# Turning the qkv weight on TensorE instead of on VectorE, in the first attention of a fused block

## The reference, cut to what matters

```python
# _L0_cond_ref: a low-rank adapter per batch entry
Bx  = jnp.einsum('bni,bri->bnr', x, B[adapter_ids])
out = jnp.einsum('bnr,bor->bno', Bx, A[adapter_ids])
# _L0_attn_ref: 32 query heads in 8 groups, each with its key and value head
qkv  = jnp.einsum('sbh,ph->sbp', tokens, weight_qkv)      # p = 8 groups * (4 + 2) heads * 128
scores = jnp.einsum('bhsd,bhtd->bhst', q, k) * scale      # causal, s and t run over 8
attn = jax.nn.softmax(scores, axis=-1)
out  = jnp.einsum('bhst,bhtd->bhsd', attn, v)
out  = jnp.einsum('sbe,he->sbh', out, weight_proj)
x = x + out
```

## Time and profile before

| | |
|---|---|
| median of 3 runs | 1549.35 us (1543.15 to 1550.29) |
| the profiled execution's own time | 1550.29 us |
| its span, first to last instruction | 1548.6 us |
| busy: PE | 1485.0 us, 96% |
| busy: DVE / ACT / POOL | 78% / 56% / 57% |
| mean granted TensorE clock | 0.989 of full speed |
| DMA | 133.37 MB, 169701 packets, of which 119187 under 512 B |
| first stage | from the start to about 290 us |

### The profile page before, as it was taken

The page is one execution under the profiler, slowest core; times in us unless marked ns, Lnnn a source line. Parts: engine busy times, 40 slices in busy tenths (PEclk is TensorE's granted clock), DMA queues, the critical chain, the costliest instruction groups (busy, mean ns, idle before and its releaser), DMA issues.

```text
span 1548.6 us, 26991 instructions
## 1 busy us (share of the span) xinstructions
PE 1485.0 (96%) x8792; PEld 1269.1 (82%) x8792; DVE 1208.1 (78%) x2700; ACT 866.8 (56%) x2260; POOL 878.9 (57%) x1231
## 2 busy tenths in 40 slices
PE   6699999989999999999999999999999999999997
PEld 4588888778888888888888888888888888888885
DVE  5688887778778887788788888878788888777865
ACT  2322232356666666666666666666666666666641
POOL 1111343256666666766676676667666766676521
PEclk9899999999999999999999999999999999999999
DMA  8988765222212221222122222212221222211102
GB/s 184 230 169 173 171 137 148 80 83 72 79 55 71 69 77 57 72 68 71 57 81 71 69 68 75 71 55 73 80 69 57 74 74 59 88 57 50 41 27 82
DMA packets 169701, 133.37 MB, mean 86 GB/s; under 512 B 119187, under 2 KB 128787, under 8 KB 169563
## 3 DMA queue, kind: packets, MB, share of 16 engines
q1 hardware_dynamic: 152098, 97.56, 23.9%
q0 software_dynamic: 16464, 33.85, 7.4%
q10 hardware_dynamic: 1000, 0.23, 0.1%
HBM read 107.47 MB, written 7.34 MB: 74 GB/s over the span
## 4 chain that ended last, share of the span: by engine, by line
PE 86%; SPq 5%; ACT 2%; issue 2%; DVE 2%; POOL 1%; DMA 1%; POOLq 0%; DVEq 0%
PE ps_t L932 14%; PE ps_o L746 11%; PE ps_o L748 11%; PE ps_o L747 10%; PE ps_b L746 5%; PE ps_b L748 5%; PE ps_b L747 5%; PE ps_q L748 4%; PE ps_q L747 4%; PE ps_q L746 4%; PE ps_a L746 3%; PE ps_a L747 3%; PE ps_a L748 3%; SPq L454 2%; PE ps_a L795 2%
## 5 line engine op out<-in xcount | busy, mean ns | idle before, releaser
L1418 ACT ACTIVATE sm<-sm,mn 128x640 f32<-128x640 f32 x256 | 211.4, 826 | 233.6 <-DVE mn L1908 227.1
L1784 DVE TENSOR_TENSOR pT_lo<-ps_t,pT_hi 128x512 fp32r<-128x512 f32 x320 | 220.2, 688 | 114.5 <-ACT pT_hi L1341 101.5
L629 POOL DMA_INDIRECT kraw<-in_L_cond_k_cache_dram,idx_a x200 | 197.4, 987 | 89.2 <-issue 75.7
L1341 ACT ACTIVATE pT_hi<-ps_t 128x512 fp32r<-128x512 f32 x320 | 188.5, 589 | 85.1 <-PE ps_t L932 82.2
L629 POOL DMA_INDIRECT vraw<-in_L_cond_v_cache_dram,idx_a x200 | 198.6, 993 | 59.6 <-issue 59.3
L932 PE MATMUL ps_t<-ident,sm 128*128 128x128 f32 x1280 | 196.4, 276 | 3.5 <-DVE sm L1920 1.5
L932 PEld LDWEIGHTS ps_t<-ident,sm 128*128 128x128 f32 x1280 | 148.7, 141 | 51.6 <-DVE qT_lo L1784 17.5
L646 POOL TENSOR_TENSOR z<-pairs_p,zl 128x128 f32<-128x128 f32 x160 | 57.9, 402 | 193.6 <-DVE pairs_p L1637 193.6
L746 PE MATMUL ps_o<-wo_lo,oT_hi 128*128 128x512 f32 x256 | 118.0, 461 | 12.4 <-ACT kvown L1345 10.8
L746 PE MATMUL ps_o<-pT_lo,v_hi 128*128 128x512 f32 x320 | 129.8, 405 | 0.0
L748 PE MATMUL ps_o<-pT_hi,v_hi 128*128 128x512 f32 x320 | 125.5, 392 | 0.0
(11 more groups left out here) (257 smaller groups left out, 4305.6 us busy)
## 6 DMA issues: line engine op xcount, KB each, us to landing
fv<-st SPq DMA_DIRECT2D x128, 128.0 KB, 2.4
tab<-tab_scratch SPq DMA_DIRECT2D x64, 256.0 KB
wblk<-n_L_attn_weight_qkv_dram SPq DMA_DIRECT2D x32, 384.0 KB
wpraw<-_L_attn_weight_proj_dram SPq DMA_DIRECT2D x8, 1024.0 KB, 5.6
mask<-mask_scratch SPq DMA_DIRECT2D x64, 128.0 KB
wtile<-in_L_cond_Wq_dram SPq DMA_DIRECT2D x28, 256.0 KB
wtile<-in_L_cond_Wo_dram SPq DMA_DIRECT2D x28, 256.0 KB
kraw<-in_L_cond_k_cache_dram,idx_a POOLq DMA_INDIRECT x200
```

The lines of the kernel that those rows point to most:

```text
L629: pool.indirect_dma_start(raw[:, par, c, :], None, rows_d, bass.IndirectOffsetOnAxis(idx[:, k:k + 1].bitcast(U32), 0)).then_inc(arrived[pa ...
L1341: act.activation(dst, src, ACT.Copy).then_inc(t_hi, 1)
L1418: act.activation(sm[:, h, :], sm[:, h, :], ACT.Exp, bias=mn[:, h:h + 1], scale=-1.0, accum_out=den[:, h:h + 1]).then_inc(e_done, 1)
L1784: dve.tensor_tensor(lo, src, hi.bitcast(F32), ALU.subtract).then_inc(t_lo, 1)
```

## The change

The load of a group becomes one DMA with rows of 512 floats into a double buffer `wraw[g % 2]`. The six tiles are turned by TensorE: `w_group(g, t)` makes four transposes into the `ps_t` ring, reading every fourth column (a stride of 16 bytes) of the tile, and ScalarE copies the bank to `wT` (`w_copy`). `wT` is now single, `fold(g, t)` waits for its own tile's copy, and VectorE's `turn` is gone. The adapters' A matrices are loaded in runs of 256 bytes, with the same change of the order of the contracted index (p * 4 + j for j * 128 + p), so that the product stays what it was. The loads for group g + 2 all stand behind the scatter of group g.

```diff
-        wraw = at("wraw", [P, 6, HID], F32, 148)
-        wblk = at("wblk", [P, NC_, 24, 32], F32, 148)
+        wraw = [at("wraw0", [P, 6, HID], F32, 148), at("wraw1", [P, 6, HID], F32, 0)]
-        wT = [at("wT0", [P, NC_, 6 * P], F32, 136), at("wT1", [P, NC_, 6 * P], F32, 0)]
+        wT = at("wT", [P, 6, NC_, P], F32, 136)
...
-        T_FIRST = ["P0", "P1", "P2", "P3"]
-        T_BOTH = ["Z0", "Z1", "P0", "P1", "Z2", "P2", "P3", "Z3", "Z4"]
+        T_FIRST = ["W0", "W1", "W2", "W3", "W4", "W5", "P0", "P1", "P2", "P3"]
+        T_BOTH = ["W0", "W1", "W2", "W3", "W4", "W5", "Z0", "Z1", "P0", "P1", "Z2", "P2", "P3", "Z3", "Z4"]
...
             def load_w(g):
-                blocks = w_qkv[g * 6 * P:(g + 1) * 6 * P, :].rearrange("(k b) (c i a) -> i b c k a", b=32, c=NC_, i=4)
-                for i in range(4):
-                    sp.dma_start(wblk[32 * i:32 * i + 32, :, :, :],
-                                 blocks[i]).then_inc(wq_in, 16)
+                sp.dma_start(wraw[g % 2][:], w_qkv[g * 6 * P:(g + 1) * 6 * P, :].rearrange("(t p) o -> p t o", p=P)
+                             ).then_inc(wq_in[g % 2], 16)
...
-                sp.dma_start(aall[:, n, :, :],
-                             lora_a[bass.ds(a_id, 1), :, :].rearrange("a (j p) r -> (a p) j r", j=NC_)
+                sp.dma_start(aall[:, n, :, :].rearrange("p j r -> p (j r)"),
+                             lora_a[bass.ds(a_id, 1), :, :].rearrange("a (p j) r -> (a p) (j r)", j=NC_)
                              ).then_inc(lora_in, 16)
+            load_w(1)
             load_wp(1)
-            sp.wait_ge(w_turned, 4)
-            load_w(1)
...
-                if g >= 1 and g + 2 < G:
-                    sp.wait_ge(w_turned, 4 * (g + 2))
-                    load_w(g + 2)
                 for h in range(HG):
                     scatter(g, h)
                 if g + 2 < G:
-                    if g == 0:
-                        sp.wait_ge(w_turned, 8)
-                        load_w(2)
+                    load_w(g + 2)
                     load_wp(g + 2)
...
+            def w_group(g, t):
+                if t == 0:
+                    pe.wait_ge(wq_in[g % 2], 16 * (g // 2 + 1))
+                raw = wraw[g % 2][:, t, :].rearrange("p (o j) -> p o j", j=NC_)
+                ring(g, f"W{t}", [raw[:, :, j] for j in range(NC_)]).then_inc(w_full, 1)
...
             def fold(g, t):
-                if t == 0:
-                    pe.wait_ge(w_turned, 4 * (g + 1))
+                pe.wait_ge(w_done, 6 * g + t + 1)
...
+            def w_copy(g, t):
+                act.wait_ge(w_full, 6 * g + t + 1)
+                act.activation(wT[:, t, :, :], ring(g, f"W{t}")[:, :].rearrange("p (c b) -> p c b", c=NC_), ACT.Copy
+                               ).then_inc(w_done, 1)
...
             for i in range(1, G):
+                for t in range(6):
+                    w_copy(i, t)
                 z_copy(i, 0)
...
             for i in range(1, G):
-                if 1 < i < G - 1:
-                    turn(i + 1)
...
-                if i == 1:
-                    turn(2, [0])
```

More of the change, by code:

```diff
@@ L230, in block_program @@
         idx_ok = sem("idx_ok")
-        wq_in = sem("wq_in")
+        wq_in = [sem(f"wq_in{i}") for i in range(2)]
         wp_in = [sem(f"wp_in{i}") for i in range(2)]
-        w_turned = sem("w_turned")
+        w_full = sem("w_full")
+        w_done = sem("w_done")
         p_full = sem("p_full")
@@ L384, in t_freed @@
             kind, j = name[0], int(name[1])
+            if kind == "W":
+                return w_done, 6 * i + j + 1
             if kind == "P":
@@ L510, in _ @@
                 if g + 2 < G:
[L511 to L513 removed]
+                    load_w(g + 2)
                     load_wp(g + 2)
                 if g == G - 2:
[L516 to L517 removed]
+                    sp.dma_start(wraw[0][:, 0:HG, :], wq[0:QW, :].rearrange("(t p) i -> p t i", p=P)
                                  ).then_inc(w0_in, 16)
[L519 to L520 removed]
+                    sp.dma_start(wraw[0][:, HG, :], wk[0:P, :]).then_inc(w0_in, 16)
+                    sp.dma_start(wraw[0][:, HG + 1, :], wv[0:P, :]).then_inc(w0_in, 16)
                     sp.dma_start(wpraw[0][:], wo[:, 0:QW].rearrange("(t p) e -> p t e", p=P)).then_inc(w0_in, 16)
@@ L784, in c_group @@
                     pe.wait_ge(w0_in, 64)
-                ring(G, f"C{t}", [wraw[:, t, c * P:(c + 1) * P] for c in range(NC_)]).then_inc(w0_full, 1)
+                ring(G, f"C{t}", [wraw[0][:, t, c * P:(c + 1) * P] for c in range(NC_)]).then_inc(w0_full, 1)
             def fold(g, t):
-                if t == 0:
-                    pe.wait_ge(w_turned, 4 * (g + 1))
+                pe.wait_ge(w_done, 6 * g + t + 1)
                 if g >= 1 and t == 0:
@@ L794, in fold @@
                 for j in range(NC_):
-                    mm = pe.matmul(ps_a[:, t * P:(t + 1) * P], wT[g % 2][:, j, t * P:(t + 1) * P], aall[:, :, j, :],
+                    mm = pe.matmul(ps_a[:, t * P:(t + 1) * P], wT[:, t, j, :], aall[:, :, j, :],
                                    start=(j == 0), stop=(j == NC_ - 1))
@@ L863, in _ @@
                 mm.then_inc(zT_full, 1)
+            w_group(0, 0)
+            w_group(0, 1)
             pe.wait_ge(zT_done, 2)
@@ L870, in _ @@
             pe.wait_ge(lora_in, 16 * N)
-            for t in range(6):
-                fold(0, t)
+            fold(0, 0)
+            w_group(0, 2)
+            fold(0, 1)
+            w_group(0, 3)
+            fold(0, 2)
+            w_group(0, 4)
+            fold(0, 3)
+            w_group(0, 5)
+            fold(0, 4)
+            fold(0, 5)
             p_group(0, 0)
@@ L892, in _ @@
             for i in range(1, G):
-                for t in range(4):
-                    fold(i, t)
+                w_group(i, 0)
+                w_group(i, 1)
+                fold(i, 0)
+                w_group(i, 2)
+                fold(i, 1)
+                w_group(i, 3)
+                fold(i, 2)
+                w_group(i, 4)
+                fold(i, 3)
+                w_group(i, 5)
                 z_group(i, 0)
@@ L1563, in tables @@
                 assert TB_ANGLES + 8 + N == TB_ALL
-            def turn(g, cs=range(NC_)):
-                for c in cs:
-                    if c == 0:
-                        dve.wait_ge(wq_in, 64 * (g + 1))
-                        if g >= 2:
-                            dve.wait_ge(fold_full, g - 1)
-                    dve.transpose(wT[g % 2][:, c, :], wblk[:, c, :, :].rearrange("p k a -> p (k a)")).then_inc(w_turned, 1)
             angles()
@@ L1577, in _ @@
             dve.memset(score[:], NEG).then_inc(smx0, 1)
-            turn(0)
             dve.wait_ge(bmask_ok, 3)
@@ L1707, in _ @@
             soft_sum(0)
-            turn(1)
             for i in range(1, G):
-                if 1 < i < G - 1:
-                    turn(i + 1)
                 z_low(i, 0)
@@ L1716, in _ @@
                 x2_sum(i, 0)
-                if i == 1:
-                    turn(2, [0])
                 x2_sum(i, 1)
-                if i == 1:
-                    turn(2, [1])
                 p_low(i, 1)
                 x2_sum(i, 2)
-                if i == 1:
-                    turn(2, [2])
                 products_s(i, 0)
@@ L1733, in _ @@
                 x2_sum(i, 3)
-                if i == 1:
-                    turn(2, [3])
                 products_s(i, 3)
```

1 line of the change is left out of this document (added).

## The result

The changed kernel takes 1563.71 us (median of four runs, 1562.99 to 1565.45), the kernel before beside it 1549.82 us (1543.15 to 1550.8): a ratio of 1.0098, with a 95% interval of 1.0078 to 1.0118. It is slower, by 13.9 us. The prediction was 1561 us.

The account below looks back on a forecast made before the run. The prediction took PE, busy for 96% of the span, as the bound. Terms of -2.7 - 5.8 + 19.4 + 0.6 = +11.5 us on 1550.29 us gave 1561.8, less 0.9 for the median: 1561 us, range 1555 to 1577.

Parts of the forecast that it names:

- The transposes: Even loop periods: 24 PE transposes of 0.111 us plus a 0.58 us wait, 3.24 us each, +19.4 over six.
- the wait: Even period: fold(i, 0) waits 0.58 us for ScalarE's copy of tile 0; later copies are hidden.
- The stride: Transposes' weight loads with a 16-byte step: nearly all hidden under the matmul before, 0.6 us in all.
- ScalarE's doubling: ScalarE copy, 578 ns contiguous, 1076 strided; argument for the dear-load rival, 1572 us, or 1580 if nothing hidden, chance 0.24.
- The first marker: First matmul of z_out(1, 0), after the group 0 to 1 crossing: forecast at 66.4 us, 2.7 us earlier.
- a clock that holds: Crossing to group 1: without PE's clock falling to 1.2 GHz, the marker of i = 1 would come at 64.8 us.
- Group 1: Period from i = 1 to i = 2: group 2's turns and their DMA waits go, -5.8 us.
- Sum: Whole kernel: -2.7 - 5.8 + 19.4 + 0.6 = +11.5 us on the profiled execution's 1550.29 us.
- The other rivals: Start of kernel and scatter: early start, 1557 us at best, chance 0.11; late start or scatter, 1564 us, chance 0.07.
- The start: Kernel start: rival that small loads land earlier, gain at most 3.8 us, 1557 us; chance 0.11.
- the scatter late: Start or scatter comes later, with group 1's weights also in flight during the start; 1564 us, chance 0.07.
- this rival: The rival that the start or the scatter comes later; 1564 us, chance 0.07.

Follow-up runs that it names:

- e1: Changed kernel with the weight transposes reading contiguous blocks of 128 columns and adapters loaded in the old order; own time 1554.79 us, before's median 1541.77 us.
- e2: Changed kernel with tile 0's transposes of the next group moved ahead of the last z_out on TensorE; own time 1552.76 us, before's median 1541.77 us.
- e6: Kernel before without VectorE's turns for groups 3 to 7, whose folds use stale tiles; own time 1540.97 us beside 1541.32 us for before.
- e11: Kernel before, unmodified, profiled again on the same chip as the changed kernel; own time 1542.38 us.
- e10: Kernel before, unmodified, profiled again on another chip; own time 1552.29 us.
- e3: Changed kernel with group 1's first three wT copies moved ahead of group 0's exponential on ScalarE; own time 1552.80 us, before's median 1541.77 us.
- e12: Changed kernel, unmodified, profiled again on the same chip as the kernel before; own time 1556.16 us.
- e0: Changed kernel, unmodified, profiled once more; 1555.18 us against 1541.32 us for before, ratio 1.0090.
- e7: Changed kernel with both tile 0's transposes ahead of the last z_out and group 1's three copies ahead of the exponential; 1550.3 us against 1541.32 for before.
- e8: Kernel before with only group 1 turned by TensorE, copies ahead of the exponential, all 16 table and mask writes behind group 0's scatter; ratio to before 1.0014.
- e9: Kernel before with only group 1 turned by TensorE, mask writes ahead of group 0's scatter, table writes behind; 1545.91 against 1552.18 us, ratio 0.9966.
- e5: Kernel before with only group 1's weight turned by TensorE and ScalarE, first three copies ahead of group 0's exponential; ratio to before 0.9972.

## Why the prediction was right, step by step

**The transposes.** Predicted 24 x 0.111 + 0.58 = 3.24 us in a period; measured 3.32 to 3.33 in the first profile of the changed kernel. Taken apart: 0.17 us the stride (`e1`), 0.44 the wait (`e2`), for which I had 0.58, and the rest, 2.72, the transposes, for which I had 2.66. The 0.1 us for PE to resume was too much: in group 1 the copy ends at 57.26 us and the fold starts at 57.30. Six periods gave 19.4 in the sum, and `e6` shows that nothing is to be set against them. This step carries the result, and it was right.

**The stride.** I took 0.6 us in all, on the argument that a load has 50 ns to spare. The load grew by 69 ns and cost 7 ns per transpose (0.17 / 24), about 1.2 us over the groups, twice the 0.6. The argument held in the main, though not its last step: a load half as slow again is 70 ns longer, which is more than the 50 to spare. ScalarE's doubling was the wrong row to scale from. The Trainium skill's rule of 16-byte lines (SBUF — State Buffer, Door 1: The DMA port swizzle) agrees with the load's own 209 against 140 ns, but nearly all of that ends under the matmul. The Trainium skill's rule of columns over 1.2 GHz for a load (TensorE: Matmul & The Clock Gate, LDWEIGHTS (loading the stationary operand)) gives 107 ns for loads that here take 140, 192 and 209.

**The first marker.** In the first pair of profiles this is the term that was mis-sized: -2.7 us, measured -0.5 (68.65 against the forecast 66.4). About 0.9 us came with the start: the fold begins at 57.30 us, for 56.4 forecast. The product of x and B lasts 9.37 us instead of 8.57, since PE's clock rose later: the granted clock from 24 to 26 us is 0.58, against 1.00 before. This is no effect of the change, because the kernel before has 0.59 there in `e11` and 0.50 in `e10`. The other 1.3 us are the clock (11.35 us from the fold to the marker, for 10.0). I let 3.3 us pass at half clock, as behind the wait of 3.60 us, but the mean granted clock from 56 to 62 us was 0.53, and 11.35 us against 8.4 at full clock is a loss of 2.95 us, for 1.6. `e3` confirms the mechanism: without the wait the clock holds. That its marker comes at 64.61 us, near the 64.8 that I had for a clock that holds, is chance: the 64.8 are a fold at 56.4 us and 8.4 us behind it, while in `e3` the fold starts at 53.88 us and, with the waits for z and for a copy, 10.73 us pass behind it.

On one chip (`e11`, `e12`) the change brings the first marker from 71.38 to 69.15 us: -2.2, near the forecast. Part of that has a cause that I had not seen. In `e11` the clock fell once more in group 0, behind a wait of PE for `wpT_lo`, and in `e12` it did not; the rows are PE's wait and the window from 42 to 46 us, first of `e11`, then of `e12`:

```profile
42.50 0.95 PE L769 MATMUL ps_t<-ident,wpraw 128*128 128x128 f32 x4 [1.69 <-DVE wpT_lo L1642]
42.00:46.00 4.00, 3.50 (x14) 3.22 (x15) 2.34 (x6) 1.19 (x2) 0.00 (x0) 0.59 1.21 241
```

```profile
43.23 0.66 PE L762 MATMUL ps_t<-ident,wpraw 128*128 128x128 f32 x4 [0.16 <-DVE wpT_lo L1657]
42.00:46.00 4.00, 3.84 (x26) 3.31 (x27) 3.02 (x7) 3.24 (x6) 0.00 (x0) 1.00 0.81 290
```

The 16 transposes between the folds of group 0 fill most of that wait. From 32 to 50 us the granted clock is 1.00 in all seven profiles of the changed kernel and its variants (`e0` to `e3`, `e7`, `e12` and the first); in the kernel before and its variants it falls once in six of seven, in `e10`, `e8` and `e9` at 34 to 36 us (0.50 to 0.52) and in `e5`, `e6` and `e11` at 44 to 46 us (0.50). Only the first profile of before, from which I forecast, has no such fall. That the filled wait is what keeps the clock up is not shown; no experiment was aimed at it, and the fall at 34 to 36 us does not stand behind that wait.

**Group 1.** Predicted -5.8 us, so a period of 36.49 - 5.8 + 3.24 = 33.9; measured 34.06. In size it depends on the execution: before had 36.49, 32.34 and 34.81 us there (the first profile, `e10`, `e11`), the changed kernel 34.06, 34.06 and 34.05 (the first, `e0`, `e12`). In `e11` and `e12` the period falls by only 0.8 us where the forecast has 2.6, so there the miss lies in this term and not in the first marker. What both pairs agree on is the sum: up to i = 2 the change gains 2.9 us in the first pair and 3.0 in `e11` and `e12`, for 5.3 forecast. I had both terms from one profile of before, whose first marker was the earliest (69.14 for 71.4 us) and whose next period the longest; that the two partly cancel is luck.

**Sum.** +11.5 us forecast; at the last marker +13.7 in the first profiles, +14.4 on one chip. The difference of 2.2 is the first marker in the first profiles. On one chip the gain up to i = 2 is 2.3 us short of the forecast, and the five periods behind it cost 17.4 us, for 16.2, since two of them are long. I set the sum on an own time of 1550.29 us that held 10 us of `kvown` waits. The medians of 1549.82 and 1563.71 us fit if the timed runs of both kernels held them too, but that is an inference, and that the 1561 came so near rests on it.

**The other rivals.** The start did not come earlier: the wait for `bsel` ended at 17.76 us instead of 17.12 (18.35 in `e12`, 17.49 in `e11`), later by 0.6 to 0.9 and nearly hidden, since PE then waits for DVE's copy anyway, until 21.11 us (20.92 before). In `e0` it ended at 19.00 us, and PE's products began at 21.38. Nor was the scatter late: its last DMA leaves at 61.48 us, seven us ahead of the marker. It was in `e5` that this rival came true.

## What to carry to other kernels

Moving work to the engine that bounds the kernel costs its full length in every round, while the wait it takes away may stand in only one. Count the rounds in which the wait stands, and change only those: here one group in eight turned a loss of 1% into a gain of 0.3%. When a wait goes, read each queue up to the point for what comes next: the copy behind the exponential, the scatter behind the table writes, and the products that wait for a buffer to be written out were each visible in the order before they took over.

## What the runs showed of the hardware that I had not expected

The difference of 10 us and more between chips is for the most part ScalarE copies that start up to 0.7 us late though the engine is idle. One such copy of `kvown` in the first profile of before, and one that is not held up, in that of after:

```profile
442.86 0.38 ACT L1345 ACTIVATE kvown<-ps_o 128x256 f32<-128x256 f32 x1 [1.18 <-PE ps_o L748]
```

```profile
456.63 0.38 ACT L1370 ACTIVATE kvown<-ps_o 128x256 f32<-128x256 f32 x1 [0.49 <-PE ps_o L741]
```

The first starts 0.73 us after the end of the last product that it copies, the second 0.04 us; the idle time ahead is 0.69 us longer, and PE then waits 0.72 us for the bank. The same shows in small in `e12`, in the copy of `mix` in two periods of the loop, 2.65 and 3.40 us behind their markers (171.31 and 205.37):

```profile
173.96 0.60 ACT L1294 ACTIVATE mix<-ps_o 128x512 f32<-128x512 f32 x1 [1.44 <-PE ps_o L804]
...
208.77 0.60 ACT L1294 ACTIVATE mix<-ps_q 128x512 f32<-128x512 f32 x1 [2.20 <-PE ps_q L804]
```

The second is idle 0.76 us longer behind the same product, and the period is 34.40 instead of 34.06 us. Of the six periods from i = 1 to i = 7 the last two or three are long in this way in `e0`, `e1`, `e2`, `e3`, `e7` and `e12`, and one in `e8` and `e10` (30.98 and 31.04 us), but none in the first profile of the changed kernel. The late copy of `mix` is shown here for `e12` alone. What holds these copies back stays open; no experiment here was aimed at it.

The clock at the start varies too, in one and the same kernel. The granted clock of the kernel before from 24 to 26 us (the third number from the end) was 1.00 in the first profile and 0.50 in `e10`:

```profile
24.00:26.00 2.00, 2.00 (x6) 0.86 (x5) 2.00 (x3) 0.00 (x0) 0.00 (x0) 1.00 1.12 341
```

```profile
24.00:26.00 2.00, 2.00 (x3) 0.79 (x3) 2.00 (x3) 0.00 (x0) 0.00 (x0) 0.50 1.09 354
```

The first marker hangs on that in part: it came at 69.14 us in the one and at 71.43 us in the other. The product of x and B ended 1.57 us later in `e10`, and the second fall of the clock, at 34 to 36 us, followed.
